# A graph transformer layer on one Trainium2 core: the mixing branch leaves the node loop and runs inside the blocks of the edge stream

## What is computed

```python
xn = _layernorm(x, axis=-1)
x = x + gnn(xn) + mix(xn)              # gnn: attention over the edges, 4 heads of 64
x = x + moe(_layernorm(x, axis=-1))    # 16 experts, top 2
...
def _L0_mix_ref(x, w_qkv, w_out, b_out):      # 8 heads of 64
    q, k, v = split(x @ w_qkv)
    k = _inst_norm(k)
    v = _inst_norm(v)
    dots = einsum('bhnd,bhne->bhde', k, v)    # a sum over all nodes
    out = einsum('bhnd,bhde->bhne', q, dots) * (1.0 / n)
    return out @ w_out + b_out
```

## Time and profile before

| | |
|---|---|
| median of 3 runs | 2571.6 us (2568.73 to 2573.27) |
| profiled execution, span from first to last instruction | 2885.5 us |
| busy in the profiled span | PE 68%, DVE 59%, ACT 49%, POOL 45% |
| mean granted clock of TensorE | 0.732 |

### The profile page before, as it was taken

How to read it: one execution, slowest core, us unless ns; L and a number is a source line. 1 busy time by engine, 2 the same in 40 slices (tenths; PEclk the granted TensorE clock), 3 DMA queues, 4 the chain that set the end, 5 groups by cost and what they waited for, 6 DMA issues and landing times. The chain is left out here.

```text
span 2885.5 us, 41185 instructions
## 1 busy us (share of the span) xinstructions
PE 1974.6 (68%) x8208; PEld 1382.7 (48%) x8209; DVE 1712.1 (59%) x3913; ACT 1407.0 (49%) x4790; POOL 1307.5 (45%) x1293
## 2 busy tenths in 40 slices
PE   4888866755246666665665666666757369999966
PEld 2555543432123333343343434343446369999954
DVE  6988798988135454544545445455678234444458
ACT  2544443332246747566565765747754124434434
POOL 2322200001735656656665565656217546666622
PEclk9999985556655656666666665657765579999987
DMA  4000000000423433333343333334153823333345
GB/s 151 21 19 19 19 6 0 0 0 10 122 85 102 112 96 108 109 106 106 102 112 99 103 110 105 108 98 112 36 176 42 115 68 106 107 101 106 104 134 165
DMA packets 133144, 245.18 MB, mean 85 GB/s; under 512 B 32277, under 2 KB 81347, under 8 KB 133009
## 3 DMA queue, kind: packets, MB, share of 16 engines
q0 software_dynamic: 54176, 140.57, 18.0%
q1 hardware_dynamic: 70190, 94.19, 11.1%
q10 hardware_dynamic: 8642, 9.08, 1.8%
HBM read 208.85 MB, written 34.88 MB: 84 GB/s over the span
## 5 line engine op out<-in xcount | busy, mean ns | idle before, releaser
L1019 POOL DMA_INDIRECT big<-feat_d,pair_idx x832 | 798.9, 960 | 552.3 <-PE wide L1144 294.1
L1144 PE MATMUL wide<-big 128*128 128x260 f32 x1664 | 757.0, 591 | 171.0 <-ACT big L1046 105.6
L1046 ACT ACTIVATE big<-big 128x64 f32<-128x64 f32 x3328 | 803.9, 336 | 16.1 <-issue 14.7
L1391 DVE TENSOR_TENSOR big<-big,wide 128x260 f32 x832 | 352.9, 424 | 580.4 <-PE wide L1144 340.0
L1144 PEld LDWEIGHTS wide<-big 128*128 128x128 f32 x1664 | 389.1, 275 | 298.9 <-ACT big L1046 186.3
L1108 PEld LDWEIGHTS wide<-score_parts,hot_t 128*128 128x128 bf16 x832 | 107.2, 129 | 347.0 <-issue 308.8
L1108 PE MATMUL wide<-score_parts,hot_t 128*128 x832 | 110.5, 188 | 199.8 <-DVE hot_t L1304 88.4
L1038 ACT ACTIVATE wide<-wide 128x4 f32<-128x4 f32 x26 | 4.1, 158 | 475.1 <-PE wide L1135 458.5
L2007 PEld LDWEIGHTS p_h<-xT,w_sb 128*128 128x128 f32 x1808 | 221.2, 193 | 8.0 <-issue 2.3
L2007 PE MATMUL p_h<-xT,w_sb 128*128 128x128 f32 x1808 | 221.7, 276 | 2.0 <-issue 2.0
L311 ACT ACTIVATE big<-big 128x896 f32<-128x896 f32 (+2 forms) x153 | 137.7, 900 | 169.9 <-DVE big L595 152.5
(11 more groups left out here) (347 smaller groups left out, 3184.7 us busy)
## 6 DMA issues: line engine op xcount, KB each, us to landing
big<-code_d SPq DMA_DIRECT2D x52, 512.0 KB
big<-in_L_ffn_w_dram SPq DMA_DIRECT2D x32, 512.0 KB
b_sb<-in_L_ffn_b_dram SPq DMA_DIRECT2D x113, 128.0 KB
big<-feat_d,pair_idx POOLq DMA_INDIRECT x832
big<-moe_d SPq DMA_DIRECT2D x7, 1792.0 KB, 9.9
feat_d<-feat_sb SPq DMA_DIRECT2D x49, 130.0 KB, 2.1
y_d<-Y ACTq DMA_DIRECT2D x7, 896.0 KB
X<-in_x_dram SPq DMA_DIRECT2D x6, 1024.0 KB, 11.9
```

The lines of the kernel that those rows point to most:

```text
L1019: nc.gpsimd.indirect_dma_start(out=rows[:, n // SB % RB, n % SB, :], out_offset=None, in_=m["feat_d"], in_offset=bass.IndirectOffsetOnAxis ...
L1046: ins = nc.scalar.activation(rows[:, b, s, cols], rows[:, b, s, cols], ACT.Copy, scale=rows[:, b, s, HF + h:HF + h + 1])
L1144: nc.tensor.matmul(sums[s % RING][:, 0:HF + H], onehot[:, s // GP % 2, s % GP, :], rows[:, b, s, :], start=True, stop=True).then_inc(summe ...
L1391: nc.vector.tensor_tensor(of, of, sums[s % RING][:, 0:HF + H], ALU.add).then_inc(added, 1)
```

## The change

The first pass and the second pass of the mixing branch, and G, move into the blocks.

- In the node loop ACT copies k and v together to `kv_sb` (`keep_kv`, one instruction of 1024), and SP stores them to DRAM (`kv_d`), and the turned tile to `xnT_d`. POOL adds b_out to X (`shift`) in place of its copy of the turned tile, and SP stores that to `xb_d`. The sums of squares, roots, scaling and products are gone from this loop. SLOT is 10.4: the 49 turns now take 134 swaps and 18 turns, and 17 swaps and 2 turns are left in `rest`. A `turn` is done in one piece, through `p_turn` and the k/v bank.
- In blocks 0 to 12 SP loads k and v of four node tiles (2 MB) a block, ACT squares them, DVE sums the squares (`sum_squares`, one instruction over 4096 at slot 8), and one block later works out the scale with 12 small instructions in place of ACT's root and scales v (`scale_v`, at slot 3); PE adds the products of one tile behind each of slots 8, 10, 12 and 14 (`dots`).
- Block 14 and 15 make G. In blocks 16 to 25 PE does the second pass for five tiles a block behind slots 8, 11 and 14 (`mix`), and DVE adds two tiles at a time to X (`add_mix`). X lends its room to k and v meanwhile, and is loaded again from `xb_d`.
- `p_arg` shares a bank with `p_z`, and in `turn_arg` the small matmul with `drop` now stands behind the wait for `arg_made`.
- More blocks are written out, outside the loops.

```diff
-    EARLY, SLOT, STATS, cost = 7.0, 4.0, 4.0, {"swap": 3.0, "sign": 0.5, "turn": 1.6}
+    EARLY, SLOT, STATS, cost = 7.0, 10.4, 4.0, {"swap": 3.0, "sign": 0.5, "turn": 4.0}
...
             for i in range(NT):
+                sp.wait_ge(t_copied, i + 1)
+                sp.dma_start(m["xnT_d"][i * P * D:(i + 1) * P * D].rearrange("(p n) -> p n", p=P),
+                             xnT_s[:, i % 2, :, :].rearrange("p b n -> p (b n)")).then_inc(t_stored[i % 2], 16)
                 sp.wait_ge(f_staged, i + 1)
                 sp.dma_start(m["feat_d"][i * P:(i + 1) * P, :], feat_sb[:, i % 2, :]).then_inc(f_stored[i % 2], 16)
...
+                sp.wait_ge(kv_staged, i + 1)
+                sp.dma_start(m["kv_d"][i * P * 2 * INNER:(i + 1) * P * 2 * INNER].rearrange("(p n) -> p n", p=P),
+                             kv_sb[:, i % KVB, :]).then_inc(kv_stored[i % KVB], 16)
...
+            for i in range(NT):
+                for entry in slots[i][0:1]:
+                    weights_back(act, entry, p_kv[i % 2])
+                stage(i)
...
+                for entry in slots[i]:
+                    copy_weights(act, entry)
+                if i + 1 < NT:
+                    copy_t(i + 1)
+                keep_kv(i)
...
+            def kv_batch(k, b):
+
+                per, n = P * 2 * INNER, len(batch(k))
+                sp.dma_start(kv[:, b, 0:n, :], m["kv_d"][ds(k * (DB * per), n * per)].rearrange("(t p n) -> p t n", t=n, p=P)
+                             ).then_inc(kv_in[b], 16)
...
+            def squares_of(k, b, turn):
+                n = len(batch(k))
+                act.wait_ge(kv_in[b], turn * 16 + 16)
+                wait_turn(act, var_made, k)
+                nc.scalar.activation(squares[:, 0:n, :], kv[:, b, 0:n, :], ACT.Square).then_inc(squared, 1)
...
                 wait_turn(pe, ex_made, 2 * k)
+                wait_apart(pe, arg_made, k + 1, crossed)
                 nc.tensor.matmul(p_arg[:, HS:HS + H], onehot[0:1, 0, 0, :], drop[:], start=True, stop=True)
-                wait_apart(pe, arg_made, k + 1, crossed)
...
+            def mixing(k, b, stage, s):
+
+                if stage == "dots" and not (isinstance(k, int) and k == 0) or isinstance(k, int) and DOTS - 1 <= k <= DOTS:
+                    i = (s - 8) // 2
+                    if s % 2 == 0 and i in batch(k - 1):
+                        dots(k - 1, 1 - b, i)
+                elif stage == "mix":
+                    if s in (8, 11, 14) and (s - 8) // 3 < len(groups(k)):
+                        mix(k, (s - 8) // 3)
...
+            def scale_v(k, b):
+                n = len(batch(k))
+                dve.wait_ge(var_made, k + 1)
...
+                for _ in range(3):
+                    chain(nc.vector.scalar_tensor_tensor(out=w, in0=y, scalar=-0.5, in1=x, op0=ALU.mult, op1=ALU.mult))
+                    chain(nc.vector.tensor_tensor(w, w, y, ALU.mult))
+                    chain(nc.vector.scalar_tensor_tensor(out=y, in0=w, scalar=1.5, in1=y, op0=ALU.add, op1=ALU.mult))
+                chain(nc.vector.tensor_tensor(rkv[:, 0:n, :], both[:, :, 0, :], both[:, :, 1, :], ALU.mult))
+                v = kv[:, b, 0:n, INNER:].rearrange("p t (h o) -> p t h o", o=64)
+                nc.vector.tensor_tensor(v, v, rkv[:, 0:n, :].unsqueeze(3).to_broadcast([P, n, MH, 64]), ALU.mult).then_inc(v_scaled, 1)
...
+            def add_mix(k, c):
+                at, n = groups(k)[c]
...
+                dve.wait_ge(mix_psum, (k - MIX) * 3 + (c + 1))
+                of = X[:, ds((k - MIX) * MB + at, n), :].rearrange("p t d -> p (t d)")
+                nc.vector.tensor_tensor(of, of, p_mix[:, 0:n * D], ALU.add).then_inc(mix_added, 1)
```

More of the change, by code:

```diff
@@ L212, in nodes_and_sort @@
     rest = plan[at:]
-    rest_swaps = [step for step, entry in enumerate(rest) if entry[0] == "swap"]
-    assert rest[0][0] == "turn" and KB * D <= 512
-    LATER = 6
-    share = len(rest) - LATER
-    tiles_at = [range(0)] * LATER + [range(-(-k * NT // share), -(-(k + 1) * NT // share)) for k in range(share)]
     def tiles_of(g):
@@ L992, in step @@
                     spread_out(2 * k + 6)
-            with sp.Fori(0, TURNS - 2) as turn:
-                for b in range(RB):
-                    step(RB * turn + b, b, turn)
-            for k in range(RB * (TURNS - 2), NSB):
-                step(k, k % RB, k // RB)
+                mix_tables(k, b, stage)
+            blocks(sp, step)
         @block.gpsimd
@@ L1147, in add_up, with dots @@
                         between(s)
-            def step(k, b, turn):
+            def dots(k, b, i):
+                if i == 0:
+                    pe.wait_ge(v_scaled, k + 1)
+                for g in range(GRP):
+                    ins = nc.tensor.matmul(p_mix[:, g * P:(g + 1) * P], kv[:, b, i, INNER + g * P:INNER + (g + 1) * P],
+                                           kv[:, b, i, g * P:(g + 1) * P], start=(isinstance(k, int) and k + i + g == 0),
+                                           stop=(isinstance(k, int) and k == DOTS - 1), skip_group_check=True)
+                if i == batch(k)[-1]:
+                    ins.then_inc(dots_done, 1)
@@ new lines, in mix @@
+            def mix(k, c):
+                at, n = groups(k)[c]
+                pe.wait_ge(mix_added, (k - MIX) * 3 + (c + 1))
+                if c == 0:
+                    late = isinstance(k, int) and k >= LATE
+                    pe.wait_ge(xt_in, (k - MIX + 1) * 16 + (16 if late else 0))
+                    pe.wait_ge(g_made, 1)
+                for i in range(at, at + n):
+                    for b in range(KB):
+                        ins = nc.tensor.matmul(p_mix[:, (i - at) * D:(i - at + 1) * D], turned_tile(k, i)[:, b * P:(b + 1) * P], G[:, b, :],
+                                               start=(b == 0), stop=(b == KB - 1))
+                ins.then_inc(mix_psum, 1)
@@ L1150, in step @@
+            def step(k, b, turn, stage):
                 more, later = there(k + 1), there(k + 2)
@@ L1394, in step, with adds @@
+            def step(k, b, turn, stage):
                 tile = tiles_of(mybir.EngineType.DVE, k * (SB // PACK), SB // PACK)
                 more, later = there(k + 1), there(k + 2)
+                def adds(slots):
+                    for s in slots:
+                        mixing(k, b, stage, s)
+                        add(k, tile, (s,))
                 if more:
@@ L1443, in _ @@
             dve.wait_ge(pair_copied, 4)
[L1445 to L1451 removed]
+            blocks(dve, step, fin, 10)
             dve.wait_ge(added, NSB * SB + RING)
```

566 lines of the change are left out of this document (276 added, 290 removed).

## The result

The kernel after took 2557.5 us (median of 4, 2554.1 to 2560.2) where before took 2570.2 (median of 4): a ratio of 0.9953, 95% interval 0.9938 to 0.9968. It is faster by half a per cent, where 1.4% slower was forecast.

A forecast was written before the change was run, and what follows sets the result against it. DVE was taken to bound the kernel up to 694 us, and hand-overs between PE, DVE and ACT the blocks. -110 + 78 + 50 + 13 + 4 = +35 us on 2571.6 gave 2607 us, range 2520 to 2690.

The forecast's parts named there:

- B to D: The forecast's three terms for the blocks and small edits, all losses: 78, 50, 13 and 4 us.
- B: Blocks with products (0 to 12): DVE's sums and scaling and PE's products lengthen 12 blocks by 6.5 us, 78 us lost.
- C: Blocks 16 to 25: the second pass's matmuls and DVE adds lengthen 10 blocks by 5 us, 50 us lost.
- D: Small edits in the blocks: the moved matmul in `turn_arg` costs 13 us, G in blocks 13 to 15 costs 4.
- A: Nodes and sort: DVE's busy time falls to 434 us, stalls add 112, stage ends at 584, a gain of 110 us.
- 18 x 2.0: In 18 turns in the node loop DVE waits 2.0 us each for ACT's late copy of weights, 36 us.
- The 35 us for turns in which PE is slower than DVE: Twelve node-loop turns with one or two swaps and no `turn`: DVE waits for PE, 35 us taken.
- The bound of 155 us for the gain: Upper bound on the gain in nodes and sort, without weights' and pace stalls.
- Rival 1: In the blocks, added matmuls hold PE's clock up; B to D cost 60 in all, 2522 us; chance 0.27.
- Rival 2: In the blocks, DVE's added work counts in full, 9.9 us in each of 12; about 2683 us; chance 0.18.
- Rival 3: Node loop paced by PE at half clock, gain only 44 us; 2673 us; chance 0.10.
- Rival 4: In the blocks, loads of k and v delay POOL's gathers, 3 us a block over 12; 2643 us; chance 0.03.

The follow-up runs named there:

- run 3: Kernel after without the sums of squares and the scaling of v on DVE (v goes into the products unscaled): 2471.8 us, 0.9595 of before.
- run 12: Kernel after with SLOT at 4.0, as before, and the rest of the change in place: 2621.3 us, 1.0172 of before.
- Run 8: Kernel after without POOL's add of b_out in the node loop: 2551.3 us, 0.9888 of before.
- Run 2: Kernel after without the mixing branch's work in the blocks (first two loads, first four tiles' products and G stay): 2435.5 us, 0.9453 of before.
- run 4: Kernel after without PE's products behind the first block and without the second pass's matmuls: 2544.0 us, 0.9869 of before.
- Run 11: Kernel after with DVE's sums of squares and scaling cut up and placed where DVE waited for PE, all three Newton steps kept: 2501.3 us, 0.9722 of before.
- before_again: The kernel before, unchanged, profiled once more at a time near its median: span 2580.0 us.
- run 6: Kernel after with every DVE add going to one fixed accumulator tile, without register instructions between adds: 2459.3 us, 0.9524 of before.

## Why the prediction was wrong

**What held.** DVE sets the node stage, and the step that took its removed work (133 us) out of its busy time had the right mechanism. The products, scaling and sums lengthen blocks 1 to 12 by 7.3 us (78 forecast for the twelve, 88 measured), all of it DVE's; block 0 adds 3.8. From the `exponents` of block 16 to the last add, ten blocks, the second pass costs 36 us where 50 were forecast: 4.6 a block in 16 to 23, nothing in 24, 2 in 25. The loads of k and v are hidden, by run 3. B to D together: 145 forecast, 128 measured. By parts blocks 0 to 12 came 14 us dearer than B had them, C came 14 cheaper and D 17, so that the sum is within 17 us is in part luck.

**The step that failed** is the sum of the stalls in A: 6 + 20 + 36 + 35 + 15 = 112, where the trace of after has 45. By terms:

- The first wait is 5.7 and the wait for keys 18.9, as forecast (6 and 20).
- "18 x 2.0" for weights behind the projection and `stage`: the order of instructions was as described, but all waits for ACT's copy are 16.7 us in 18 waits, the first's 5.7 among them, and the 18 turns in the loop have 7.1 us in place of 36. PE and ACT were sooner than priced. From PE's first transpose of a `turn` to the end of ACT's first copy of weights the forecast had 6.2 us, and after has 4.6 on average; DVE's third pass ends 4.5 us behind the same point, where 4.2 were forecast. The 0.25 us a transpose was a mean of the earlier trace rows over a stage whose rest ran at a clock of 0.53; in the twelve turns that the trace has at 1.00 ACT's copy ends 3.6 to 4.4 us behind the start, and DVE waits at most 0.16. In the six at 0.50 to 0.66 the copy ends behind 4.9 to 6.7 us, and DVE waits 0.77 to 1.53. One turn of each kind in after, the first at a clock of 0.50 and the second at 1.00:

```profile
162.07 1.51 PE L589 MATMUL p_turn<-ident,big 128*128 128x128 f32 x6 [5.98 <-issue]
167.92 0.86 ACT L313 ACTIVATE big<-big 128x784 f32<-128x784 f32 x1
168.81 1.03 DVE L538 COPY_PREDICATED big<-big 128x784 f32<-128x784 uint32 x1 [1.53 <-ACT big L313]
...
171.51 0.85 PE L589 MATMUL p_turn<-ident,big 128*128 128x128 f32 x6 [0.31 <-issue]
174.69 0.95 ACT L313 ACTIVATE big<-big 128x896 f32<-128x896 f32 x1
175.67 1.19 DVE L538 COPY_PREDICATED big<-big 128x896 f32<-128x896 uint32 x1
```

- The 35 us for turns in which PE is slower than DVE are not there: the gaps ahead of the first pass of a swap are 0.11 us at most, 5.6 us in 148, and outside the turns and the first wait DVE waits some 4 us for ACT's copies of weights. DVE's swaps never wait for k and v, only for copies of weights behind `stage`, and buffers let PE work ahead in full turns; that this is what hides the short turns is read from the program, and no run takes the buffers away. I priced each short turn by itself, as if a barrier stood behind it. With SLOT at 4.0 (run 12), where many turns in a row are short, that cost appears: 90.5 us of waiting.
- The 15 us for barrier, signs and statistics: some 3.

One term was missing on the other side. DVE's busy time up to the last swap was to be 434 us and is 464; 21.4 of the 30 are passes made longer beside POOL, which the prediction called hidden ("POOL gives a copy and gets an add"). Run 8 gives back 16 of them. Where the last 9 come from stays open. In all the stage ended at 547 and not at 584: 37 us more gain. The bound of 155 us for the gain does not follow from its own terms: without the stalls of weights and pace they give 110 + 36 + 35 = 181.

**D** was too dear: 13 for `turn_arg` and 4 for G, and blocks 13 to 15, which carry just these, are as long as before. Run 2, which keeps the matmul behind the wait, has before's block lengths. No run puts the matmul back by itself.

37 from A and 17 from the blocks turn +35 into -19; the profiled spans differ by 21.5 (2580.0 - 2558.5), the medians by 12.7.

**The rivals.** Rival 1 would have been right in sign, but by its own mechanism it falls: the clock was higher with the products and the blocks no shorter (run 4). It put B to D at 60; they cost 128. Rival 2 (9.9 us a block in full) was nearer for the blocks than thought: 7.3 of 9.9. Run 11 shows that 4.2 of these 7.3 us hang on the places of DVE's work, and the other 3.2 on its amount. Rival 3 falls: the loop's clock was 0.86, and PE did not set its pace. Rival 4 falls by run 3.

**Readings that did not carry over.** The blocks of 49.4 us and the 580 us of idle time before adds in the earlier trace rows go with a clock of 0.66 in the blocks; in `before_again`, at 0.76, blocks 1 to 12 take 40.5 us and DVE's idle time before adds is 315.9 us. Block 24, which has no lookups, took 34.5 us there, and from that I read that the slots with lookups pace a block; in `before_again` it takes 41.3, no less than the others. Of DVE's idle time much is none: some 10 us a block, by the estimate of run 6, are register and semaphore instructions between adds. I read the 22 us a block of the earlier trace rows as room to absorb DVE's new work. By that estimate the room was some 4 us of 40, and run 11 fits in 8.4 us of work for 3.2 us of length, so 5.2. It sits in slots 1 to 5 and 28, where PE is the slower one.

## What to carry to other kernels

Where an engine's work is many short instructions with computed addresses, take the interval between two of them where nothing can hold it up, not the busy time: 0.42 us busy was 0.68 to 0.79 here, and an engine busy for 659 of 1049 us had a tenth to an eighth free. If work must be added to such an engine, cut it into pieces near the length of the wait that stands in a slot, and put each where the trace has the engine waiting for another: the same work cost 7.3 us a block in two lumps and 3.2 in pieces. And price a loop's short turns together with the full ones around them, as far as its buffers reach, before calling each a stall; and take the price of PE's part at the clock of the stretch it will run in, not as a mean over a stage with both levels.

## What the runs showed of the hardware

Passes of DVE with two operands in SBUF took 1.11 us in place of 0.58 when POOL's add of 256 columns lay beside them (28 third passes of a swap in after), and 0.74 in place of 0.59 where a swap's first pass lay beside its subtract-and-multiply (32). Of the 36 second passes beside either, 34 are not longer (0.57 to 0.59 on average), and two that began beside the add alone take 1.14. POOL's subtract-and-multiply takes 1.87 us on average in place of 1.40 before; the 11 in after that lie beside no pass of a swap take 1.37. Without the add the sort ended 16 us earlier. An add of DVE with a computed address came 0.68 to 0.79 us behind the last one, and 0.53 with a fixed address, at the same 0.42 us busy. And PE's granted clock was 0.77 in place of 0.70 with 16 small matmuls more in each block, without a gain in time.
